# A recurrent block with long convolution and eight-expert FFN: the kernel rewritten around a two-block convolution, token-layout experts and an early router, with ScalarE normalising x

## The reference, cut to what matters

```python
xn = _layernorm(x, axis=-1)
# branch 1: a gated long convolution
uv = silu(xn @ uv_w); u, v = split(uv, 2)          # 128 features each
h = pos @ rpe_pos_w                                # pos = 0, 1..511, -511..-1
for i in range(3):
    h = silu(_ln(h, ln_w[i], ln_b[i])) @ fc_w[i]   # 32 features
t = silu(_ln(h, out_ln_w, out_ln_b)) @ out_w       # t_neg, t_pos scaled by 0.99 ** |pos|
s = (u * conv_over_tokens(t, v)) @ o_w             # by FFT of length 1024 in the reference
# branch 2: experts chosen once per batch
rw = softmax(xn.mean(axis=1) @ Wr + br)            # per batch, 8 experts
w, i = top_k(rw, 2); w = softmax(w)
h = gelu(xn @ W1[i] + b1[i])                       # 512 hidden, exact gelu
f = sum_j w_j * (h_j @ W2[i_j] + b2[i_j])
g = silu(_layernorm(f + xn) * gamma + beta)
out = x + s * g
```

## Time and profile before

| | us |
|---|---|
| median of 3 runs (lowest, highest) | 260.24 (257.44, 264.85) |
| span of the profiled execution | 255.3 |
| TensorE matmul busy, 928 records | 216.9 (85%) |
| VectorE busy, 373 instructions | 136.8 (54%) |
| GpSimd busy, 105 | 106.1 (42%) |
| ScalarE busy, 172 | 99.8 (39%) |
| DMA | 19.71 MB, 77 GB/s on average |

### The profile page before, as it was taken

The page is one execution under the profiler, slowest core; times in us unless marked ns, Lnnn a source line. Parts: engine busy times, 40 slices in busy tenths (PEclk is TensorE's granted clock), DMA queues, the critical chain, the costliest instruction groups (busy, mean ns, idle before and its releaser), DMA issues.

```text
span 255.3 us, 3013 instructions
## 1 busy us (share of the span) xinstructions
PE 216.9 (85%) x928; PEld 157.9 (62%) x928; DVE 136.8 (54%) x373; ACT 99.8 (39%) x172; POOL 106.1 (42%) x105
## 2 busy tenths in 40 slices
PE   0457987758949999999895999999999999999950
PEld 0336977755625787767564778777757667756640
DVE  2999956414170300666787288548674452533374
ACT  2225556737637524332232222332262444353400
POOL 0555534061492400358996024229865205301310
PEclk9999999955988999999999999999999999999995
DMA  7317600335263230020203310420415404010011
GB/s 208 90 58 261 277 0 3 98 112 150 89 175 154 82 85 0 5 77 0 50 32 87 80 41 3 123 82 1 125 32 155 105 0 126 0 41 0 0 41 41
DMA packets 25015, 19.71 MB, mean 77 GB/s; under 512 B 1368, under 2 KB 22528, under 8 KB 24616
## 3 DMA queue, kind: packets, MB, share of 16 engines
q1 hardware_dynamic: 24624, 19.23, 25.2%
q10 hardware_dynamic: 376, 0.30, 0.5%
HBM read 17.43 MB, written 2.10 MB: 76 GB/s over the span
## 4 chain that ended last, share of the span: by engine, by line
PE 62%; DVE 16%; POOL 7%; issue 7%; ACT 4%; DMA 3%; SPq 1%; POOLq 0%; DVEq 0%; ACTq 0%
PE bank L1080 19%; PE bank L1111 10%; PE bank L924 8%; PE bank L925 8%; PE bank L926 8%; PE bank L1003 3%; PE bank L1135 2%; DVE xn L684 2%; DVE prod L727 2%; DVE stats L665 2%; POOL layer_r L578 2%; DMA x_ring<-in_L_attn_x 1%; POOL w_lo L610 1%; PE bank L1123 1%; DMA w_raw<-in_L_ffn_W 1%
## 5 line engine op out<-in xcount | busy, mean ns | idle before, releaser
L499 ACT ACTIVATE h_ring<-bank,b_sel 128x512 f32<-128x512 f32 x64 | 43.9, 688 | 67.8 <-PE bank L926 67.7
L1080 PE MATMUL bank<-h_ring,w_s 128*128 128x512 f32 x128 | 66.6, 604 | 0.0
L924 PE MATMUL bank<-xT_hi,w_hi 128*128 128x512 f32 x64 | 41.4, 647 | 0.7 <-ACT h_ring L499 0.7
L610 POOL TENSOR_TENSOR w_lo<-w_raw,w_hi 128x512 fp32r<-128x512 f32 x16 | 21.0, 1334 | 37.2 <-ACT w_hi L453 37.2
L1111 PE MATMUL bank<-inv_sb,Y 128*128 128x256 f32 x128 | 29.3, 380 | 3.7 <-DVE conv L870 2.5
L1111 PEld LDWEIGHTS bank<-inv_sb,Y 128*128 128x128 f32 x128 | 24.0, 190 | 10.6 <-issue 5.7
L1080 PEld LDWEIGHTS bank<-h_ring,w_s 128*128 128x128 f32 x128 | 24.7, 193 | 6.6 <-issue 1.0
L926 PE MATMUL bank<-xT_hi,w_lo 128*128 128x512 f32 x64 | 26.1, 408 | 0.0
L925 PE MATMUL bank<-xT_lo,w_hi 128*128 128x512 f32 x64 | 26.1, 408 | 0.0
L602 POOL TENSOR_TENSOR Y<-prod 128x512 f32<-128x512 f32 x8 | 10.9, 1365 | 35.3 <-DVE prod L862 35.3
L858 DVE TENSOR_TENSOR prod<-bank,A_sb 128x512 f32<-128x512 f32 x8 | 5.5, 692 | 29.2 <-PE bank L926 29.2
(11 more groups left out here) (153 smaller groups left out, 429.0 us busy)
## 6 DMA issues: line engine op xcount, KB each, us to landing
x_ring<-in_L_attn_x SPq DMA_DIRECT2D x16, 256.0 KB, 3.6
w_raw<-in_L_ffn_W SPq DMA_DIRECT2D x16, 256.0 KB, 2.8
w_s<-in_L_ffn_W SPq DMA_DIRECT2D x16, 256.0 KB, 2.9
Y<-table_lag SPq DMA_DIRECT2D x1, 2048.0 KB, 9.2
out_dram<-x_ring SPq DMA_DIRECT2D x8, 256.0 KB, 2.3
inv_sb<-table_fwd SPq DMA_DIRECT2D x1, 1024.0 KB, 4.8
inv_sb<-table_inv SPq DMA_DIRECT2D x1, 1024.0 KB, 4.7
c<-table_c ACTq DMA_DIRECT2D x1, 202.0 KB, 2.8
```

The source lines that it names most:

```text
L499: nc.scalar.activation(h_ring[:, n % NH], H_PS[n % 2][:], ACT.Gelu, bias=b1_sel[:, c, j, b:b + 1]).then_inc(h_done, 1)
L610: nc.gpsimd.tensor_tensor(w1_lo[:, b % 2, j], w1_raw[:, j], w1_hi[:, b % 2, j], ALU.subtract).then_inc(w1_split, 1)
L924: nc.tensor.matmul(out_ps, w_hi, m_hi, start=start, stop=False)
L1080: nc.tensor.matmul(OUT_PS[:], w2_s[:, b % 2, j, c], h_ring[:, n % NH], start=False, stop=(i == HT - 1)).then_inc(w2_mm, 1)
```

## The change

The program is written anew; only the arithmetic of the reference stays. What is different:

- **Order.** Each engine has a table of places per job (`PE_AT`, `ACT_AT`, `POOL_AT`, `DVE_AT`, `SP_AT`), sorted into one list. x and xn of all batches stay in SBUF, so x is loaded once and not again for the result.
- **Router.** Groups of batches (0), (1), (2, 3), (4 to 7) instead of all eight. Batch 0's mean comes from x and its inverse root by four matmuls of one column, before anything is transposed. Softmax's exponentials come from Tanh. The biases are picked by VectorE.
- **Normalising.** VectorE for batch 0; ScalarE for batches 1 to 7 (`ACT.Identity` with scale and bias, 4 instructions of 128x128 each), for which GpSimd does two more small instructions per batch.
- **Experts.** `expert_out` takes `h_ring` as weights and `w2_s` as moving operand: 4 fp32 matmuls of 128 columns for one of 512. The sum stands tokens by features, so the unit-matrix matmuls, ScalarE's copy and the transposes back are gone; xn plus the mixed b2 is added by GpSimd (`residual`) and VectorE (`experts_out`). ScalarE scales W2, and normalises y for 7 batches. The low part of W1 is made by VectorE and GpSimd in turns.
- **Convolution.** Two blocks of 256 tokens, transform length 512. Forth: 8 pieces (2 batches, 2 halves of the frequencies) of 4 fp32 matmuls of 256 columns. Three products instead of one: `product` is called three times per piece, 6 multiplications of 128x512 and one sum on VectorE, 5 additions of 128x512 on GpSimd. Back: 8 fp32 matmuls of 128 columns per batch. The filter's spectrum needs 2 transposes, 2 matmuls of 512 columns and 8 of 256 or 384.

```diff
-LAYER_AT = [3, 7, 11]
-ROUTER_AT = B
+GROUPS = [(0, 1), (1, 2), (2, 4), (4, 8)]
+NXT, NRAW, NSPLIT, NW2, NH = 6, 3, 4, 4, 4
+XN_ON = ["dve"] * 1 + ["act"] * 7
...
+    "h": [19, 20, 23, 25, 32, 34, 37, 38, 41, 42, 45, 46, 48, 51, 54, 58, 59, 62, 63, 66, 90, 92, 93, 95, 99,
...
-            pe.wait_ge(sel_done, 1)
-            pe.wait_ge(v_done, B)
-            hidden(0)
-            hidden(1)
...
+            def first_mean(n):
+                pe.wait_ge(rstd_done, 1)
+                pe.wait_ge(wrc_done, 1)
+                for t in range(NT):
+                    last = nc.tensor.matmul(R0_PS[:, 8:9], x_all[:, 0, t], rstd[:, 0, t:t + 1],
+                                            start=(t == 0), stop=(t == NT - 1))
+                last.then_inc(mean0_ps, 1)
...
+            def normalize(b):
+                act_e.wait_ge(rstd_done, b + 1)
+                for t in range(NT):
+                    last = nc.scalar.activation(xn[:, b, t], x_all[:, b, t], ACT.Identity,
+                                                bias=xnb[:, b, 1, t:t + 1], scale=rstd[:, b, t:t + 1])
+                last.then_inc(xn_act, 1)
...
-                nc.tensor.matmul(OUT_PS[:], w2_s[:, b % 2, j, c], h_ring[:, n % NH],
-                                 start=False, stop=(i == HT - 1)).then_inc(w2_mm, 1)
+                for t in range(NT):
+                    tok = slice(t * P, (t + 1) * P)
+                    last = nc.tensor.matmul(OUT_PS[b % 2][:, tok], h_ring[:, n % NH, tok], w2_s[:, i % NW2, c],
+                                            start=(n % HT == 0 and t == 0), stop=(n % HT == HT - 1),
+                                            skip_group_check=True)
+                last.then_inc(out_ps, 1)
...
+            def forth(m, n, ps):
+                q, kc = m // 2, m % 2
+                for ri in range(2):
+                    last = nc.tensor.matmul(ps[:, ri * BLK:(ri + 1) * BLK], fwd_sb[:, ri, kc],
+                                            fold[:, q, ri, n].rearrange("p b d -> p (b d)"),
+                                            start=True, stop=True)
+                return last
...
+            def product_both(m):
+                dve.wait_ge(v1_done, m + 1)
+                dve.wait_ge(p3_done, m + 1)
+                nc.vector.tensor_tensor(V0_PS[:], V0_PS[:], v1_s[:], ALU.add).then_inc(sum_done, 1)
+                dve.wait_ge(sum_done, m + 1)
+                product(m, 0, V0_PS[:]).then_inc(p1_done, 1)
...
-                nc.gpsimd.tensor_tensor(Y[:, q % KC, 0], prod[:, 0], prod[:, 2], ALU.subtract)
-                nc.gpsimd.tensor_tensor(Y[:, q % KC, 1], prod[:, 1], prod[:, 3],
-                                        ALU.add).then_inc(Y_done, 1)
+            def spectra(m):
+                q, kc = m // 2, m % 2
+                pool.wait_ge(p1_done, m + 1)
+                step(nc.gpsimd.tensor_tensor(prod[:, 0], prod[:, 0], prod[:, 1], ALU.add))
...
+                for n, with_third in ((0, 2), (1, 4)):
+                    last = nc.gpsimd.tensor_tensor(Y[:, q % 2, kc, n].rearrange("p r b d -> p (r b d)"),
+                                                   prod[:, 0], prod[:, with_third], ALU.add)
+                last.then_inc(Y_done, 1)
```

More of the change, by code:

```diff
@@ L56 @@
 PW = 2 * S // RG
[L57 removed]
 HT = TOPK * FC
+NTILE = B * TOPK
 EPS = 1e-5
 GAMMA = 0.99
[L66 to L85 removed]
@@ L551, in _ @@
+            for what, n in in_order(ACT_AT):
+                jobs[what](n)
         @block.gpsimd
@@ L652, in _ @@
+            for what, n in in_order(POOL_AT):
+                jobs[what](n)
         @block.vector
@@ L915, in _ @@
-            jobs = {"w2": w2_scale, "eps": layer_eps, "spread": layer_spread, "layer": layer_norm,
-                    "products": products, "conv": convolved, "split": split_fold,
-                    "sum": gate_sum, "norm": gate_norm, "affine": gate_affine, "result": result}
-            for what, n in DVE_JOBS:
+                    last = nc.vector.scalar_tensor_tensor(out=z_s[:, b % 2, t], in0=y_s[:, b % 2, t],
+                                                          scalar=ymv[:, b, t, 0:1], in1=gam[:],
+                                                          op0=ALU.subtract, op1=ALU.mult)
@@ L919, in _ @@
+            for what, n in in_order(DVE_AT):
                 jobs[what](n)
@@ new lines, in logits @@
+            def logits(g):
+                first, end = GROUPS[g]
+                if g == 0:
+                    pe.wait_ge(mean0_done, 1)
+                    nc.tensor.matmul(R0_PS[:, 16:16 + E], bcast(mean0[:], [P, P]), wrc[:], start=True,
+                                     stop=True).then_inc(logit_ps, 1)
+                else:
+                    pe.wait_ge(xlo_done, end)
+                    for b in range(first, end):
+                        last = nc.tensor.matmul(RT_PS[:, (b - first) * E:(b - first + 1) * E],
+                                                bcast(xsum[:, b:b + 1], [P, P]), wrc[:], start=True, stop=True)
+                    last.then_inc(logit_ps, 1)
@@ L1055, in hidden, with feature_spectra @@
-            def hidden(n):
-                b, j, c = n // HT, n % HT // FC, n % FC
-                if n % FC == 0:
-                    pe.wait_ge(w1_split, n // FC + 1)
+                    last = nc.tensor.transpose(A_PS[:, cc * P:(cc + 1) * P], act[:, cc * P:(cc + 1) * P], ident)
+                last.then_inc(phi_ps, 1)
+            def feature_spectra(n):
+                pe.wait_ge(phi_done, 1)
+                pe.wait_ge(lag_in, 16)
+                for cc in range(2):
+                    last = nc.tensor.matmul(A_PS[:], phiT[:, cc], lag_sb[:, cc], start=(cc == 0), stop=(cc == 1))
+                last.then_inc(cs_ps, 1)
@@ L1105, in transform_back, with back @@
+            def back(b):
+                q, s = b // 2, b % 2
+                pe.wait_ge(Y_done, 2 * q + 2)
                 if b == 0:
                     pe.wait_ge(inv_in, 16)
[L1107 removed]
+                    pe.wait_ge(logit_read, len(GROUPS))
+                else:
                     pe.wait_ge(eo_read, b)
[L1109 to L1113 removed]
@@ L1172 @@
+            for what, n in in_order(PE_AT):
+                jobs[what](n)
 NAMES = ["L0_attn_x", "L0_attn_uv_w", "L0_attn_o_w", "L0_attn_rpe_pos_w", "L0_attn_rpe_ln_w",
```

1581 lines of the change are left out of this document (838 added, 743 removed), and 21 rows, old and new, of tables (DVE_AT, PE_AT, POOL_AT, SP_AT).

## The result

The changed kernel takes 220.9 us (median of 4 runs, 219.9 to 221.5), the kernel before 262.4 (median of 4, 257.4 to 264.9; it was 260.2 with the runs shown ahead of the prediction). The kernel before has, now and then, runs some per cent slower than its others, as 264.6 and 264.9 here, and the ratio is taken without those: it is 0.852, with a 95% interval of 0.845 to 0.859, faster by 15%. The forecast was 210 and the range 197 to 227, so the time is inside it and 11 us above the forecast. The profiled execution has a span of 219.3 us where the sum said 205: 14.3 us are to be explained.

What follows compares the result with a forecast made beforehand. A late router choice, then TensorE's own work, was taken to bound the kernel; front 31, middle 56, last part 101.5 + 4 and tail 12.4 gave 205, forecast 210 as a median, 8 in 10 within 197 to 227.

Steps and rivals of the forecast that it cites:

- the sum: Whole kernel: 31 + 56 + 101.5 + 4 + 12.4 = 205 us, against a span of 255.3 before.
- TensorE's prices at full clock: Matmul prices from the earlier trace: W2 product 0.89 against 0.86, forth matmuls of 256 columns 0.43, back 0.22 per 128 columns.
- The front, 31: Start to first hidden matmul: router index at 22, W1 at 26.5, first hidden at 31; bounds 27 and 36.
- The middle, 56: First hidden to first transform: TensorE 52.5 and ScalarE 52 us, not wholly overlapping, so 56; bounds 53 and 64.
- ScalarE's normalising, 0.27 per 128x128: Normalising x on ScalarE: 0.27 us per instruction, extrapolated from wider ones, 7.6 in all; bounds 0.15 and 0.385.
- The last part, 105.5: First transform to last expert product: TensorE 101.5 us, GpSimd 102 with contention, VectorE 90, plus 4 for waits.
- The tail, 12.4: Behind the last expert product: 14.3 us before, less ScalarE's copy and four transposes (1.1 and 0.8), gives 12.4.
- From span to median, 4.9: Whole kernel: the earlier median was 4.9 us above the profiled span, so a span of 205 became 210.
- All smooth: Whole kernel: front 27, middle 53, no waits, so span 194 and median 199; chance 0.12.
- GpSimd becomes the bound: Last part: GpSimd needs 117 us where TensorE needs 101.5, at 1.61 per 128x512; median 226; chance 0.15.
- The clock falls: Last part: repeated waits hold TensorE at its low level, 50 us more, 255; chance 0.04, half of it slower.
- The early choice gains nothing: Middle: VectorE and ScalarE are late anyway, it stretches from 56 to 75, median 229; chance 0.03.

## Why the prediction was right, and where it was off

**Faster, and in the range: right.** 0.96 stood on it, by the mechanism named: choice and first experts leave the front's end (37 instead of 57 us), and the full loop is shorter. By the stages of both profiles the front gave 19.5 us, the stretch from the first hidden to the last product 19.2, and the tail took 2.6 back. No run undoes the early choice, the exchanged roles or the shorter convolution by itself, so this division is read from the traces and not tested. The rest of what the prediction listed came too: in the last part GpSimd was busy for 89% and VectorE for 83% of the time (89.5 us where the sum had 90).

**TensorE's prices at full clock: right.** A product with W2, 4 matmuls of 128 columns and so 8 records, takes 0.89, as taken from `mixed`; and the 2.5 times of the page's ratio (the Trainium skill, TensorE: Matmul & The Clock Gate, Back-to-back issue gap) didn't come, for fp32. Chain, after:

```profile
43.34 0.89 PE bank L1216 x8
```

The transforms forth are 32 matmuls of 256 columns, 64 records at 0.22, so 0.43 each and 13.8 us, as taken. In the last part TensorE is busy for 104.9 us where the terms gave 101.5; about 1.7 of the difference is the low clock behind the hole.

**The front, 31: wrong by 6.2, and outside my bounds of 27 and 36.** The failed step is "v and u of batch 0 (2.0)" and its like: prices of the full clock, put on a stretch where TensorE runs at the low level. From 20.05 to 24.75 v, u and logits of batch 0 take 4.7 us, and the index came at 24.9, not 22; another 4.7 go to batch 1 in the same way, and v of batch 2 takes 2.8 from 33.8 on, just ahead of the first hidden. These three alone are about half as long at the high level, 5 to 6 us. That low rate showed in the earlier trace rows, where I used it for a rival of the last part only, and in the front of the kernel before ahead of 30.8, where I didn't look. Added matmuls showed it to be a cause: 3.1 us of the front and 1.5 more behind it came back; for v and u of batches 0 and 1 nothing did in that run, since the clock had fallen again.

**The middle, 56: right in sum.** My picture of it was not. ScalarE was to be level with TensorE at 52 us; it is busy for 44.6 of 56.8, and TensorE for 56.2. TensorE's terms of 52.5 were about right: of its 56.2, some 3 are the first 6 us at half rate. My 3.5 for handovers happened to cover that, which is luck.

**ScalarE's normalising, 0.27 per 128x128: too cheap.** Groups by line, after:

```profile
L562 ACT ACTIVATE xn<-x_all,xnb,rstd 128x128 f32<-128x128 f32 x28 | 11.4, 482 | 6.9 <-POOL xnb L639 6.9
```

Four take 1.65 us in a row, 0.41 each, above even my upper bound of 0.385: a price taken from other shapes of the line's neighbours. One alone takes 0.48, more than a 128x256 copy; it also reads a scale and a bias per partition, which the copy doesn't, and no run separates the two. "Hidden where TensorE or VectorE is late" held for batches 1 and 2 (4.3 us gained) and not for the others (1.7 us lost).

**The last part, 105.5: nearly right, by a shared bound.** The prediction had GpSimd at 102 beside TensorE at 101.5; the rows have 96.3 and 104.9, and the cuts on one and on both bear out that they are level. Of the 4 us of waits 3.5 are there, but 2.3 of them in one place, the hole; I had spread them over the pieces. Another 1.7 is the low clock behind it. What the step missed is that contention doesn't only stretch 128x512 instructions by a quarter or by double: it can hold a 4-element one for as long as GpSimd's instruction lasts. Three of the chain (`share`, `mix`) lost 2.5 us so, and a `b_mix` pair of 2.73 us stood in front of `cw`. This chain was in no term.

**The tail, 12.4: wrong by 4.5.** I took the old tail less what was removed, and put "two back and two `mixed`" under it at no cost. The failed step is that the tail is VectorE's, and that this work brings VectorE more than it lost: 13.0 us busy of 16.9, against 8.3 of 14.3. The convolution, gate and result of batch 6 stand in it beside those of batch 7, some 2.9 us more; the residual sum of batch 7 is new there (0.7); and normalising with gamma and beta takes 4.4 us where it took 2.7 before (timeline of VectorE, before):

```profile
246.78 1.36 DVE L886 TENSOR_SCALAR zb<-bank,ymv,yrstd 128x128 f32<-128x128 f32 x4
248.17 0.69 DVE L894 TENSOR_TENSOR zb<-zb,gam 128x512 f32<-128x512 f32 x1
```

The last is contention: of the new eight instructions of 128x128 the first four take 3.24 us beside GpSimd's affine of batch 6 and the next four 1.14 without. GpSimd had 1.27 us of work in the old tail and has 5.19 now. Moving the affine to GpSimd gained nothing; doing batch 6's share before the last product wasn't tried.

**From span to median, 4.9: too much.** The first median, 260.2, was of runs up to 7 us apart, and a span of 255.3 fits the quickest of them (257.4). In the profiled run of the changed kernel time and span are 221.1 and 219.3, 1.8 apart. This term gave back some 3 us of the 14.3 that the sum of the stages was short, so the 11 us by which the forecast is off look better than the sum does.

**The rivals.** *All smooth* is out. *GpSimd becomes the bound* has come true by half: level, with 1.3 to 1.5 us per 128x512 instead of 1.61. *The clock falls* stayed small in the last part: low from 111.3 to 114.7 and in the tail. In the front the level was low, where I hadn't looked for it. *The early choice gains nothing* is out.

## To carry to other kernels

A price from the full loop doesn't hold where an engine has just been idle: take the front's prices from rows of the front, by the spacing of like matmuls, since a granted clock of 1.00 ahead of the first rise says nothing. Compare profiles only after looking where the clock rose and fell in each. When two engines slow each other, keep small instructions on which others wait out of the other's long ones; a reordering of four numbers was worth 1.7%. And when one engine is cut and little comes back, cut the next one as well before judging: two engines at 93 and 99.7% give their gain only together.
